# Edge tiles of 125 or 128 rows, and how many tiles are gathered, in a five-pass graph network kernel

## The reference

```python
h = relu(layernorm(x))                                   # before every layer
# layer 0 (pass l0): NNConv, edge features 16 wide
w_edge = (relu(edge_attr_16 @ W1 + b1) @ W2 + b2).reshape(-1, 16, 16)
out = segment_sum(einsum('ei,eio->eo', h[src], w_edge), dst) + h @ root + bias
x = x + relu(batchnorm(out))
# layer 1 (pass l1): rows of dst are gathered, sums go to src
m = silu(einsum('ei,ej,ijh->eh', h[dst], edge_attr_8, W_msg) * c) @ W_lin
agg = segment_sum(m, src);  x = x + h + silu(einsum('ni,nh,ihk->nk', h, agg, W_upd) * c) @ W_upd_lin
# layer 2 (passes l2a, l2b): relational convolution with 8 edge types, twice
agg = segment_sum((h[src] @ W[edge_type]) / count[dst, edge_type], dst) + h @ root + b
x = x + log_softmax(second)
# layer 3 (pass l3)
x = x + segment_sum((h * out_deg ** -0.5)[src], dst) * in_deg ** -0.5
```

## Time and profile before

| | |
|---|---|
| median of 3 runs | 4559.57 us (4553.13 to 4559.76) |
| profiled execution | 4555.6 us, of which the span of instructions is 4553.4 us |
| mean granted TensorE clock | 0.983 of full speed |
| PE, DVE, ACT, POOL busy | 95%, 91%, 71%, 72% of the span |
| steady stretches | l0 120 to 1400 us, l1 1520 to 2300, l2a 2420 to 3100, l2b 3180 to 3855, l3 3945 to 4530 |

### The profile page before, as it was taken

How to read it: one execution, slowest core, us unless ns; L and a number is a source line. 1 busy time by engine, 2 the same in 40 slices (tenths; PEclk the granted TensorE clock), 3 DMA queues, 4 the chain that set the end, 5 groups by cost and what they waited for, 6 DMA issues and landing times.

```text
span 4553.4 us, 107759 instructions
## 1 busy us (share of the span) xinstructions
PE 4339.6 (95%) x30477; PEld 3261.8 (72%) x30477; DVE 4121.4 (91%) x11864; ACT 3235.6 (71%) x5359; POOL 3284.9 (72%) x2515
## 2 busy tenths in 40 slices
PE   4999999999997999999979999998999999799998
PEld 3777777777775777777747777776777777566665
DVE  5999999999997999999969999997999998888887
ACT  3777777777774777777737777775777777677776
POOL 4888888888883777777727777775777775688886
PEclk8999999999998999999989999999999999899999
DMA  3111111111111222222211111111111111111111
GB/s 72 21 17 18 17 18 17 18 18 18 18 17 40 61 59 61 59 60 60 59 37 27 27 28 27 27 28 39 27 28 28 26 28 23 30 31 31 30 31 24
DMA packets 336556, 148.67 MB, mean 33 GB/s; under 512 B 250040, under 2 KB 322532, under 8 KB 336392
## 3 DMA queue, kind: packets, MB, share of 16 engines
q0 software_dynamic: 104000, 59.31, 10.1%
q1 hardware_dynamic: 232517, 88.88, 7.8%
HBM read 135.45 MB, written 9.80 MB: 32 GB/s over the span
## 4 chain that ended last, share of the span: by engine, by line
PE 81%; DVE 10%; issue 5%; ACT 2%; DMA 1%; SPq 1%; DVEq 0%; POOL 0%; POOLq 0%; ACTq 0%
PE acc L600 37%; PE rows_ps L757 16%; PE rows_ps L693 7%; PE bank L773 5%; PE bank L693 4%; PE counts L607 3%; PE eaT_ps L765 3%; DVE raw L1258 2%; PE rows_ps L681 2%; DVE stationary L1234 2%; PE eaT_ps L669 1%; DVE one_hot L1206 1%; PE counts L604 1%; DVE rows_ps L1321 1%; ACT stack L928 1%
## 5 line engine op out<-in xcount | busy, mean ns | idle before, releaser
L600 PE MATMUL acc<-one_hot,stationary 125*128 125x392 bf16 x12000 | 2335.4, 329 | 39.5 <-DVE stationary L1234 35.1
L584 POOL DMA_INDIRECT gathered<-table_l,row_numbers x1200 | 1607.3, 1339 | 461.1 <-issue 349.1
L600 PEld LDWEIGHTS acc<-one_hot,stationary 125*128 125x128 bf16 x12000 | 1157.3, 100 | 709.0 <-DVE stationary L1234 49.9
L866 ACT ACTIVATE distances<-count_hi,fields 125x392 bf16<-125x392 f16 (+1 forms) x2500 | 1227.5, 560 | 0.0
L1234 DVE TENSOR_TENSOR stationary<-mask,parts 125x1024 bf16<-125x1024 bf16 x1500 | 943.3, 683 | 0.3 <-ACT mask L851 0.2
L851 ACT CAST mask<-is_lo 125x1024 bf16<-125x1024 f32 x500 | 523.1, 1046 | 447.3 <-DVE is_lo L1187 393.5
L584 POOL DMA_INDIRECT fields_all<-table_l,row_numbers x500 | 646.3, 1293 | 259.6 <-issue 114.8
L1206 DVE TENSOR_SCALAR one_hot<-count_hi,fields 125x392 bf16<-125x392 f16 x2300 | 734.4, 341 | 13.5 <-issue 13.5
L1321 DVE COPY_PREDICATED rows_ps<-near_bits_now,rows_ps 125x320 f32<-125x320 int8 (+3 forms) x1600 | 579.7, 362 | 162.6 <-PE rows_ps L757 118.6
L584 POOL DMA_INDIRECT gathered<-table_l2a,row_numbers x400 | 512.7, 1282 | 282.6 <-DVE parts L1216 119.4
L757 PE MATMUL rows_ps<-node_parts,h1T 125*125 125x192 bf16 (+1 forms) x7200 | 678.3, 252 | 27.0 <-DVE node_parts L1285 19.6
(11 more groups left out here) (213 smaller groups left out, 4706.6 us busy)
## 6 DMA issues: line engine op xcount, KB each, us to landing
near_key<-near_keys_by_chunk SPq DMA_DIRECT2D x300, 122.1 KB
gathered<-table_l,row_numbers POOLq DMA_INDIRECT x1200, 2.8
fields<-edge_fields SPq DMA_DIRECT2D x500, 31.2 KB
near_key<-near_keys_by_chunk SPq DMA_DIRECT2D x100, 91.6 KB
fields_all<-table_l,row_numbers POOLq DMA_INDIRECT x500, 3.5
gathered<-table_l2a,row_numbers POOLq DMA_INDIRECT x400
gathered<-table_l2b,row_numbers POOLq DMA_INDIRECT x400
ea<-in_edge_attr SPq DMA_DIRECT2D x100, 62.5 KB
```

The lines of the kernel that those rows point to most:

```text
L584: pool.indirect_dma_start(out=gathered[ph][:, s, t, :], in_=table[ph], out_offset=None, in_offset=bass.IndirectOffsetOnAxis(ap=row_numbers ...
L600: mm = pe.matmul(acc[:, :], stationary[:, s, k, t, :, :].rearrange("p a b -> p (a b)"), one_hot[:, s, t, :], start=first and t == 0 and k ...
L866: ins = act.activation(distances[:, i * n:(i + 1) * n], count_hi[:, 0:n], ACT.Abs, scale=-1.0, bias=fields[:, s, k, t:t + 1].bitcast(F32))
```

## The change

The tile becomes 128 edges high. 100,000 edges don't fill whole chunks of 1024: there are 98 chunks, of which 54 are whole (`WHOLE`); the last 44 are read from a view that begins 352 edges earlier, so that partition 0 there holds duplicates, whose source and destination DVE overwrites with nodes that do not exist. Loops of SP are split at chunk 54 for that. Then:

- Near tiles: l1 3 to 2, l2a and l2b 4 to 3, l3 stays 4. So far tiles are 8, 6, 5, 5, 4 a chunk instead of 8, 5, 4, 4, 4.
- Loads of near keys go to 128 partitions. `near_ea8` is loaded per chunk, behind a wait for the outer product of the chunk two before (`near_outers`).
- x is loaded as 96 partitions, 1 partition and the rest. `ident` and the small weights come ahead of the edges; the edges are six loads (whole and ragged part of three arrays); the row numbers of chunks 0 and 1 come with the first edge features.
- On DVE the diagonals and the fields come first, and the near keys after `rooted`. PE turns the near keys inside chunk 0, before its edge weights; ACT copies them there. `near_work` lies in slot 1 of `stationary`.
- The fields are stored in five pieces (chunks 0 to 3, 4 to 11, 12 to 39, 40 to 69, 70 to 97), issued at the start and after chunks 1, 2, 4 and 6, and SP waits for two of them at chunk 4 and for all at chunk 9.

```diff
-EP, T = 125, 8
+EP, T = 128, 8
 E = 100000
-TILES = E // EP
-CHUNKS = TILES // T
+CHUNKS = -(-E // (EP * T))
+TILES = CHUNKS * T
+PADDING = EP * TILES - E
+WHOLE = CHUNKS - PADDING // T
+WHOLE_EDGES = EP * WHOLE * T
-NEAR_OF = {"l0": (0, 0), "l1": (3, 3), "l2a": (4, 4), "l2b": (4, 4), "l3": (4, 4)}
+NEAR_OF = {"l0": (0, 0), "l1": (2, 2), "l2a": (3, 3), "l2b": (3, 3), "l3": (4, 4)}
...
-        near_key = sb("near_key", [NEAR_NP, 2, NEARS * EP], F16)
+        near_key = sb("near_key", [128, 2, NEARS * EP], F16)
-        near_ea8 = sb("near_ea8", [EP, CHUNKS, NEAR1 * RELATIONS])
+        near_ea8 = sb("near_ea8", [EP, 2, NEAR1, RELATIONS])
...
+        EVEN = FULL // 16 * 16
+        as_nodes = [(slice(0, EVEN), slice(0, LOCAL), slice(0, EVEN * LOCAL)),
+                    (slice(EVEN, FULL), slice(0, LOCAL), slice(EVEN * LOCAL, FULL * LOCAL)),
                     (slice(FULL, NP), slice(0, REST), slice(FULL * LOCAL, N_NODES))]
+        FIELD_PIECES, FIELDS_STORED_AT = (4, 12, 40, 70, CHUNKS), (1, 2, 4, 6)
+        def by_rows(v):
+            names = "(p c t) f -> p c t f" if len(v.shape) == 2 else "(p c t) -> p c t"
+            return (v[0:WHOLE_EDGES].rearrange(names, p=EP, t=T),
+                    v[WHOLE_EDGES - PADDING:].rearrange(names, p=EP, t=T))
...
+            for into, k in ((src, "src"), (dst, "dst"), (typ, "edge_type_8")):
+                whole, ragged = by_rows(A[k])
+                sp.dma_start(into[:, 0:WHOLE * T], whole.rearrange("p c t -> p (c t)")).then_inc(ev("edges_in"), 16)
+                sp.dma_start(into[:, WHOLE * T:], ragged.rearrange("p c t -> p (c t)")).then_inc(ev("edges_in"), 16)
...
+                if ph == "l1":
+                    if later(chunk, 2):
+                        sp.wait_ge(near_outers, chunk - 1)
+                    sp.dma_start(near_ea8[:, s].rearrange("p t r -> p (t r)"),
+                                 rows_of(ea8_d, chunk, ragged, (T - NEAR1) * RELATIONS)).then_inc(near_key_in[s], 16)
...
-                    if chunk == 1:
-                        store_fields(slice(4, CHUNKS))
+                    if chunk in FIELDS_STORED_AT:
+                        n = FIELDS_STORED_AT.index(chunk)
+                        store_fields(slice(FIELD_PIECES[n], FIELD_PIECES[n + 1]))
+                    if chunk == 1 + LO:
+                        sp.wait_ge(ev("fields_stored"), 16 * len(FIELD_PIECES))
...
-                            sp.dma_start(near_ea8[:], ea8_d[:, :, (T - NEAR1) * RELATIONS:]).then_inc(ev("diagonals_in"), 16)
...
+                    pe.wait_ge(ev("near_keys_made"), 1)
+                    keys = near_work[0].bitcast(F32)
+                    for j in range(KEYS):
+                        into, at = (bank[4], j) if j < NEARS else (bank[3], j - NEARS)
+                        mm = pe.transpose(into[0:CHUNKS, at * EP:(at + 1) * EP], keys[:, :, j], ident[0:EP, 0:EP])
+                    mm.then_inc(ev("near_keys_in_psum"), 1)
                     pe.wait_ge(ev("near_keys_turned"), 1)
                 edge_weights(chunk)
```

More of the change, by code:

```diff
@@ L188, in build @@
         near_outerT = h1_room[:, NEARS * EP:2 * NEARS * EP]
-        near_work = [h1_room[0:EP, i * CHUNKS * KEYS:(i + 1) * CHUNKS * KEYS].bitcast(I32).rearrange(
-            "p (c k) -> p c k", c=CHUNKS) for i in range(2)]
         near_is_type = sb("near_is_type", [EP, NEARS, RELATIONS])
@@ L211, in build @@
         stationary = sb("stationary", [EP, 2, 3, T, LO, F], BF16)
+        near_work = [stationary[:, 1].rearrange("p k t a f -> p (k t a f)").bitcast(F32)[:, i * CHUNKS * KEYS:(i + 1) * CHUNKS * KEYS].bitcast(I32).rearrange(
+            "p (c k) -> p c k", c=CHUNKS) for i in range(2)]
+        near_work.append(product[:].rearrange("p a b c d -> p (a b c d)")[:, 0:CHUNKS * KEYS].bitcast(I32).rearrange(
+            "p (c k) -> p c k", c=CHUNKS))
         zeros = sb("zeros", [EP, HI + W], BF16)
@@ L277, in build, with near_keys_in_by @@
         near_done = sem("near_messages_ready")
+        def near_keys_in_by(ph, pair):
+            return 32 * (pair + 1) if ph == "l1" else 16 * (PAIRS + chunks_before(ph) // 2 + pair + 1)
         def far(ph, s):
@@ new lines, in _, with rows_of @@
+            ea_d = [v.rearrange("p c t f -> p c (t f)") for v in by_rows(A["edge_attr_16"])]
+            ea8_d = [v.rearrange("p c t f -> p c (t f)") for v in by_rows(A["edge_attr_8"])]
+            rows_d = {ph: by_rows(A[k]) for ph, k in (("l0", "src"), ("l1", "dst"), ("l3", "src"))}
+            def rows_of(views, chunk, ragged, first=0):
+                view, at = (views[1], chunk - WHOLE) if ragged else (views[0], chunk)
+                return view[:, bass.ds(at, 1), first:].rearrange("p c n -> p (c n)")
@@ L407, in store_fields, with load_ea @@
+            def load_ea(chunk, s, ragged=False):
+                sp.dma_start(ea[:, s].rearrange("p t f -> p (t f)"),
+                             rows_of(ea_d, chunk, ragged)).then_inc(ea_in[s], 16)
             def store_fields(chunks):
@@ L424, in later_copies, with load_numbers @@
                     sp.dma_start(bd[k][rows, lo, :, :], A[w].rearrange("r i o -> i r o")).then_inc(ev("diagonals_in"), 16)
-            def load_numbers(ph, chunk, pair, s):
+            def load_numbers(ph, chunk, pair, s, ragged=False):
                 if later(chunk, 2):
@@ L459, in stream_near, with body @@
             def stream_near(ph):
-                def body(chunk, pair, s):
-                    load_numbers(ph, chunk, pair, s)
+                def body(chunk, pair, s, ragged):
+                    load_numbers(ph, chunk, pair, s, ragged)
                     if later(chunk, 2):
@@ L514, in stream_l0 @@
                         later_copies(chunk - 2)
-                with sp.Fori((2 + LO) // 2, PAIRS) as pair:
-                    for s in range(2):
-                        body(2 * pair + s, pair, s)
+                for first, end in (((2 + LO) // 2, WHOLE // 2), (WHOLE // 2, PAIRS)):
+                    with sp.Fori(first, end) as pair:
+                        for s in range(2):
+                            body(2 * pair + s, pair, s, end == PAIRS)
             def store_table(ph, stage, where):
@@ L528, in store_quarters @@
                     sp.dma_start(where[:, c * n:(c + 1) * n], stage[:, c * n:(c + 1) * n]).then_inc(table_in, 16)
-            for s in range(2):
-                load_numbers("l0", s, 0, s)
             store_table("l0", stage0[:].rearrange("p l f -> p (l f)"), table0.rearrange("(p l) f -> p (l f)", p=NP))
@@ L647, in _ @@
             times("l0_root_made", bank[2], "root")
-            pe.wait_ge(ev("near_keys_made"), 1)
-            keys = near_work[0].bitcast(F32)
-            for j in range(KEYS):
-                into, at = (bank[4], j) if j < NEARS else (bank[3], j - NEARS)
-                mm = pe.transpose(into[0:CHUNKS, at * EP:(at + 1) * EP], keys[:, :, j], ident[0:EP, 0:EP])
-            mm.then_inc(ev("near_keys_in_psum"), 1)
             pe.wait_ge(ev("ident16_made"), 1)
@@ L944, in l0 @@
                     hi_one_hots("l0", chunk - 1, 1 - s, later(chunk, 3))
+                else:
+                    turn_near_keys()
                 if not last:
@@ L1275, in l0 @@
                 st.mark(matches(key_mask[:, s], count_key, s, DST_KEY, WIDE_LO * RELATIONS))
+                if s == 1 and not later(chunk, 2):
+                    dve.wait_ge(ev("near_keys_in_psum"), 1)
                 to_stationary("l0", chunk, s, parts, lambda: st.wait("low"))
```

138 lines of the change are left out of this document (71 added, 67 removed).

## The result

The changed kernel took 5319.66 us, the median of 4 runs (5313.92 to 5332.43); the kernel before took 4559.65 us in its 4 runs beside them. The ratio is 1.1675, 95% interval 1.1649 to 1.17: slower by 17%, where 4290 us and a gain of 6% were forecast, and outside the range of 4190 to 4490 us. The later runs will show that this isn't the whole result: the same kernel, unchanged, took 4246.58 us in one run of a later session.

What follows compares the result with a forecast made beforehand. PE was taken to bound l1 and l2, a PE, DVE, ACT loop l0 and l3, with POOL's room deciding the change. From 4555.6 us, -22 - 61 - 138 - 13 - 31 = -265 gave 4290 us; range 4190 to 4490.

Steps and rivals of the forecast that it cites:

- The list of rivals: Four alternatives: gather price kept, 4652 us; far cheaper gather, 4257; late row numbers in l1, 4390; little prologue gain, 4310.
- Price of a gather: On POOL, a gather over 128 rows would take 0.97 us, a fifth off 1.21; the weakest step.
- Rival 1: Gather keeps its price, so POOL bounds l1 and l2: slower by 96 us, 4652 us; chance 0.15.
- l0: Pass without near tiles: 98 chunks of 13.42 us against 100 of 13.37, -22 us.
- l1: Pass going to six gathers a chunk: 8.04 us of POOL, 788 us against 849, -61 us.
- that belongs to DVE's instructions and so stays: Stretch of POOL's gathers beside DVE's work, a fixed amount per chunk: 0.42 us in l1, 0.28 in l2a.
- l2a and l2b: Passes going to five gathers a chunk: 6.7 us a chunk, 657 us against 726, -69 us, twice.
- the floor of 6.65: Least time of an l2 chunk in us: PE's 6.44 plus 0.2 for handovers, taken from l3.
- l3: Pass keeping its near tiles: two chunks of 6.43 us less, -13 us; a cheaper gather brings nothing.
- Prologue: Start of the kernel: first product 18 us earlier and SP's wait at chunk 4 gone, 13 us; together -31 us.
- Extra SP work in l1: SP's wait before loading near features costs nothing; up to 1 us a chunk, +98 us, if cover is gone.
- The reading of the packets: In l3, 32 packets a gather fit 16 engines, so 128 rows might cost near the old price.

Runs made afterwards that it cites:

- e1: The changed kernel with the loads of near keys back to 125 partitions instead of 128; 5305.0 us.
- e4: The kernel before with its gathers over 128 partitions, the last three rows being padding that nobody reads; 5444.0 us.
- first profile: The profile that came with the first result, of the changed kernel as built; a run of 5315.23 us.
- e17: The changed kernel, unchanged, run again in a later session; 4246.6 us.
- e3: The kernel before with near keys loaded to 128 partitions instead of 125; 4556.4 us.
- e14: The kernel before with 128-row gathers; from each pass's third chunk SP skips near keys in l2a, near keys and fields in l2b, all loads in l3; 4521.2 us.
- e18: The kernel of e14, unchanged, run again side by side with e17; 4523.8 us.
- e13: The kernel before with one to three of each chunk's gathers at 128 rows and the others at 112; 4522.1 us.
- e8: The changed kernel with tiles of 125 edges, 100 chunks and the near tiles of before, keeping the new prologue and load order; 4512.3 us.
- e11: The kernel of e8 with gathers over 126 partitions, the last row being padding that nobody reads; 4479.0 us.
- e9: The changed kernel with gathers taking 126 of the 128 rows; 4340.6 us.
- e6: The kernel before with gathers of 127 rows in l0, 126 in l1, 96 in l2a, 64 in l2b and 112 in l3; 5811.0 us.
- e16: The kernel of e11 with 3 and 2 near tiles in alternate chunks of l1 and 3 in l2; 4399.3 us, ratio 0.9664.

## Why the prediction was wrong

**What failed.** No term of the sum explains +760 us. What failed is a premise under all of them: that a gather costs POOL's time and nothing else, so that POOL's room, PE's stream and DVE's stream decide ("all hangs on the price of a gather"). The list of rivals was built on it, and none has a mechanism that holds the other engines up while POOL goes on. In the first result and on the chip of e1 to e4 that happened with gathers of 128 rows: in the first profile 1181 us of waits end with an unknown source, and each pass is longer than in e17. e3 and e4 show that there it isn't the height of SP's loads, and that three padding rows a gather are enough to bring it on. e14, e17 and e18 show that the same gathers, and the very same kernel, run without it elsewhere.

**What stays open.** Why the same program stalls in one place and not in another, and by which path, isn't settled: the records name no source. Whether it belongs to the chip for good or to a session can't be told, as the five groups of runs had five chips, the first result's isn't named, and what else ran beside the kernel isn't recorded. Nor is it shown that 112 to 126 rows avoid it, since on the chips with the stall only 125 and 128 rows were run. How the loss grows with the number of such gathers wasn't measured, as e13 met no stall. The record has a hint: the lengths of the table, taken as differences and divided by the gathers of the pass, give nearly the same loss for a gather in two different kernels (first profile less e17, and e4 less e18, whose l0 and l1 do the same work and whose l2a leaves out a load of SP): 0.27 and 0.30 us in l0, 0.28 and 0.22 in l1, 0.57 and 0.50 in l2a. So the loss of a gather seems to depend on what the pass does beside it more than on the kernel; one run each is all there is for it.

**The sum itself** can be read from e17. Forecast 4290, measured 4246.6. Term by term, from the windows above (time x gathers per chunk / gathers):

- Price of a gather: 0.97 forecast, 0.940 measured. The number was right, and far from the 1.15 us at which the sign would turn; its reason wasn't (see below), so this was luck. Rival 1 had no ground.
- l0: 13.42 forecast, 1180 x 8 / 710 = 13.30 measured: -12 us over 98 chunks.
- l1: 8.04 forecast, 760 x 6 / 547 = 8.34 measured: +29 us. POOL is the bound, without idle time but its 0.30 us: 6 x (593.63 / 547 + 0.305) = 8.34. The mis-sized term is the part of a chunk "that belongs to DVE's instructions and so stays": 0.42 us forecast, 6 x (1.085 - 0.940) = 0.87 measured. It doesn't stay, and a sixth gather doesn't only add its share: the mean stretch of one gather was 0.09 us before, 0.05 in e18 (5 gathers of 128 rows, 0.986 less 0.938 us) and 0.145 here, where POOL has no pause.
- l2a and l2b: 6.7 forecast, 6.47 and 6.62 measured: -23 and -8 us. PE is busy 579.93 of 580 us, so the floor of 6.65 that I took from l3's handovers was too high.
- l3: 6.43 forecast ("A cheaper gather brings nothing here"), 6.27 measured, -16 us. The cheap gather does bring something: with 125 edges a tile l3 fell from 642.8 (e8) to 625.2 us (e11) by it alone.
- Prologue: -31 forecast, and -29 to -31 measured in e8 (by the first gathers of l1 and l3). In e17 the first gather starts at 20.0 us (forecast 27.6), the first product at 33.7 (forecast 40, before 58.54), the SP wait of 21.58 us is gone, and DVE's near keys lie under the first gathers as said.
- Extra SP work in l1: nothing forecast, nothing measured (e8, 846.7 for 847.4 us).
- The store of the result: a term at nothing, since the prediction took x's new pieces (96 partitions, 1 and the rest) for a matter of its load. The store has the same pieces. From its first issue to the end of the span 10.8 us pass before (4542.62 to 4553.4) and 2.7 us in e17 (4242.05 to 4244.7): -8 us.

The sum closes by the starts of the passes' first gathers, before 36.6, 1451.2, 2371.0, 3125.9 and 3882.6 us, and in e17 20.0, 1379.6, 2269.1, 2934.4 and 3614.8. To l1 the kernel gained 72 us (53 forecast, prologue and l0), then 30 in l1 (61), 90 in l2a (69), 76 in l2b (69) and 41 in l3 and behind it (13). Against the forecast that is -19 + 31 - 21 - 7 - 28 = -44, and 4290 - 44 = 4246. So the working was sound to 1% where nothing disturbs, its error in l1 having hidden part of the others, and was off by 24% where something does. Both numbers are the kernel's time. The first result is slower, and that is what the kernel would have cost its user there.

**The reading of the packets** was wrong too. I took the 32 packets of each gather for 16 engines with equal shares, and so for a price that need not fall. The number of packets is 32 in l2 with 126 rows as well (13,906 for 435 gathers of e9) and with 64 (11,427 for 359 of e6), so with such short rows it doesn't show how they are shared. The trace of before could have: its rows of 544 B in l1 left 80 packets a gather (36,787 for 460), where those of 128 rows left 32 in e17 (17,448 for 547). POOL's queue before, 1520 to 2300 us, which is in none of the rows (packets, MB, share):

```profile
q0 software_dynamic: 36787, 31.81, 18.2%
```

And the trace keeps the size of every packet. A gather of 125 rows of 64 B has five packets of 1600 B, which are 25 rows each, and eleven of 100 B; one of 126 rows has fourteen of 576 B (9 rows) and two of 36 B (e9); one of 128 has sixteen of 512 B (8 rows, e17). So 125 rows went to 5 engines, and not to 16 as the prediction read. The guess of a fifth less came out for another reason, below.

## What to carry to other kernels

Time a changed transfer on more than one chip before the kernel is built around it: here the same change was worth +17% or -7%, with not a byte of the kernel changed between the two. In a trace, look at who waits for nobody: pauses inside a run of matmuls, and waits with an unknown source on several engines at once, are a disturbance and no term of the plan. Pad a gather to a row count that many engines can share: one row that nobody reads took the shortest gather from 1.21 to 0.99 us, and 33 us off the kernel. e16 is the version here that beats the kernel before (by 3.4%) without gathers of 128 rows, though it wasn't run on a chip that stalls.
